# The order of the three split products in a projection, and the place of one wait, in a fused attention and feed-forward kernel

## The reference

```python
x = L0_attn_x
x = x + _layernorm(_L0_attn_ref(_layernorm(x, axis=-1), Wq, bq, Wk, bk, Wv, bv, Wo, bo), axis=-1)
x = x + _layernorm(_L0_ffn_ref(_layernorm(x, axis=-1), ...), axis=-1)
```

## Time and profile before

| | |
|---|---|
| median of 3 runs | 1695.01 us |
| lowest, highest | 1693.71, 1697.49 us |
| the profiled execution, its own time | 1693.71 us |
| its span, first to last instruction | 1691.9 us |
| mean granted TensorE clock | 0.995 |
| TensorE matmuls busy | 1657.7 us, 98% of the span, 22550 matmuls |
| TensorE weight loads busy | 1320.2 us, 78%, 22550 loads |
| DVE, ACT, POOL busy | 1310.4, 855.8, 1284.9 us |

### The profile page before, as it was taken

The page is one execution under the profiler, slowest core; times in us unless marked ns, Lnnn a source line. Parts: engine busy times, 40 slices in busy tenths (PEclk is TensorE's granted clock), DMA queues, the critical chain, the costliest instruction groups (busy, mean ns, idle before and its releaser), DMA issues.

```text
span 1691.9 us, 55468 instructions
## 1 busy us (share of the span) xinstructions
PE 1657.7 (98%) x22550; PEld 1320.2 (78%) x22550; DVE 1310.4 (77%) x2455; ACT 855.8 (51%) x1730; POOL 1284.9 (76%) x1303
## 2 busy tenths in 40 slices
PE   8999999999999999999999999999999999999994
PEld 5787887778787877878787877887788787877873
DVE  7677877778777778778777787787787787777777
ACT  4355554544555555445445445455554554454453
POOL 5577878778778778777787787787787787777867
PEclk9999999999999999999999999999999999999998
DMA  7666666566666666666666666666666666666653
GB/s 266 147 168 166 174 183 175 170 174 189 170 168 183 176 165 181 182 171 169 184 174 170 172 188 173 166 190 172 170 185 175 167 179 180 169 171 173 172 137 95
DMA packets 388635, 293.46 MB, mean 173 GB/s; under 512 B 296854, under 2 KB 296854, under 8 KB 388380
## 3 DMA queue, kind: packets, MB, share of 16 engines
q1 hardware_dynamic: 345552, 223.02, 49.7%
q10 hardware_dynamic: 42828, 66.90, 13.2%
HBM read 155.46 MB, written 67.24 MB: 132 GB/s over the span
## 4 chain that ended last, share of the span: by engine, by line
PE 94%; DVE 2%; issue 1%; DMA 1%; ACT 1%; POOL 1%; ACTq 0%; SPq 0%; DVEq 0%
PE ps_k L1080 8%; PE ps_v L1081 7%; PE ps_v L1083 7%; PE ps_v L1080 7%; PE ps_k L1081 7%; PE ps_y L1161 7%; PE ps_y L1160 7%; PE ps_k L1083 7%; PE ps_y L1164 7%; PE ps_q L1081 7%; PE ps_q L1083 7%; PE ps_q L1080 7%; PE ps_s L1121 6%; PE ps_o L1140 5%; DMA v_key<-v_d 0%
## 5 line engine op out<-in xcount | busy, mean ns | idle before, releaser
L910 ACT ACTIVATE q_sb<-ps_q,mr 128x512 f32<-128x512 f32 x127 | 87.4, 688 | 550.7 <-issue 541.5
L403 POOL TENSOR_TENSOR z<-z,b_row 128x512 f32<-128x512 f32 x124 | 187.7, 1534 | 222.1 <-DVE z L679 222.1
L605 DVE STREAM_TRANSPOSE qT<-q_sb 128x512 f32<-128x512 f32 x128 | 137.5, 1074 | 111.8 <-ACT q_sb L910 111.6
L1080 PE MATMUL ps_k<-wk_hi,xT_hi 128*128 128x512 f32 x504 | 212.1, 421 | 0.0
L1081 PE MATMUL ps_k<-wk_lo,xT_hi 128*128 128x512 f32 x504 | 199.3, 395 | 1.1 <-issue 1.1
L1160 PE MATMUL ps_y<-wo_hi,oT_hi 128*128 128x512 f32 x504 | 199.1, 395 | 0.8 <-ACT oT_hi L926 0.8
L383 POOL TENSOR_TENSOR x_t<-x_t,mr_row 128x512 f32<-128x512 f32 x126 | 195.8, 1555 | 4.6 <-ACT mr_row L1002 4.6
L1081 PE MATMUL ps_q<-wq_lo,xT_hi 128*128 128x512 f32 x504 | 199.3, 395 | 0.0
L1081 PE MATMUL ps_v<-wv_lo,xT_hi 128*128 128x512 f32 x504 | 199.3, 395 | 0.0
L1161 PE MATMUL ps_y<-wo_lo,oT_hi 128*128 128x512 f32 x504 | 199.3, 395 | 0.0
L1080 PE MATMUL ps_q<-wq_hi,xT_hi 128*128 128x512 f32 x504 | 199.1, 395 | 0.0
(11 more groups left out here) (189 smaller groups left out, 3723.4 us busy)
## 6 DMA issues: line engine op xcount, KB each, us to landing
x_in<-in_xa SPq DMA_DIRECT2D x64, 512.0 KB, 5.2
x_t<-in_xt SPq DMA_DIRECT2D x64, 512.0 KB, 4.9
k_bd<-kT SPq DMA_DIRECT2D x512, 64.0 KB, 2.5
v_d<-v_tok ACTq DMA_DIRECT2D x128, 256.0 KB, 2.0
v_key<-v_d SPq DMA_DIRECT2D x128, 256.0 KB, 3.9
res<-in_xr SPq DMA_DIRECT2D x64, 512.0 KB, 5.3
p_bd<-pT ACTq DMA_DIRECT2D x508, 64.0 KB, 2.5
out<-o_sb SPq DMA_DIRECT2D x62, 512.0 KB, 2.9
```

Of the source, the lines that this page charges most:

```text
L403: nc.gpsimd.tensor_tensor(z[:, j, :], z[:, j, :], b_row[:, :], ALU.add).then_inc(z_done, 1)
L605: nc.vector.transpose(qT[t % 2][:, :, :].rearrange("p n h -> p h n"), q_sb[:, :].rearrange("p (h d) -> p h d", d=D)).then_inc(qT_done, 1)
L1080: nc.tensor.matmul(ps, x_hi[:, e, :], w_hi[:, e, :], start=e == 0, stop=False)
```

## The change

`project` loses its second branch: tiles 1 to 127 now take the order that tile 0 had, three passes over the four chunks, hi*hi, then lo*hi, then hi*lo. `output` does the same three passes for tiles 0 to 126, with its wait for oT_lo moved ahead of its first matmul; the last tile (NT - 1) does hi*hi, hi*lo, lo*hi, and waits for oT_lo between the second pass and the third. The number of matmuls, their shapes, operands and banks are the same.

```diff
             def project(t, k, ps, w_hi, w_lo, ready):
                 x_hi, x_lo = xT_hi[t % 2], xT_lo[t % 2]
                 n = order.index(k)
-                if t == 0:
-                    for i, (x, w) in enumerate(((x_hi, w_hi), (x_lo, w_hi), (x_hi, w_lo))):
-                        if i == 1:
-                            pe.wait_ge(first_low, 1)
-                        for e in range(EC):
-                            if e % 2 == 0 and i != 1:
-                                pe.wait_ge(w_split if i else w_cast, 2 * n + e // 2 + 1)
-                            mm = nc.tensor.matmul(ps, x[:, e, :], w[:, e, :], start=i == 0 and e == 0, stop=i == 2 and e == EC - 1)
-                else:
-
+                for i, (x, w) in enumerate(((x_hi, w_hi), (x_lo, w_hi), (x_hi, w_lo))):
+                    if t == 0 and i == 1:
+                        pe.wait_ge(first_low, 1)
                     for e in range(EC):
-                        nc.tensor.matmul(ps, x_hi[:, e, :], w_hi[:, e, :], start=e == 0, stop=False)
-                        nc.tensor.matmul(ps, x_hi[:, e, :], w_lo[:, e, :], start=False, stop=False)
-                    for e in range(EC):
-                        mm = nc.tensor.matmul(ps, x_lo[:, e, :], w_hi[:, e, :], start=False, stop=e == EC - 1)
+                        if t == 0 and e % 2 == 0 and i != 1:
+                            pe.wait_ge(w_split if i else w_cast, 2 * n + e // 2 + 1)
+                        mm = nc.tensor.matmul(ps, x[:, e, :], w[:, e, :], start=i == 0 and e == 0, stop=i == 2 and e == EC - 1)
                 mm.then_inc(ready, 1)
...
                     pe.wait_ge(w_split, 8)
                     pe.wait_ge(vtok_done, 2)
-                o_hi, o_lo, to = oT_hi[t % 2], oT_lo[t % 2], y_bank.get(t, ps_y[:, :])
-                for a in range(EC):
-                    nc.tensor.matmul(to, o_hi[:, a, :], wo_hi[:, a, :], start=a == 0, stop=False)
-                    nc.tensor.matmul(to, o_hi[:, a, :], wo_lo[:, a, :], start=False, stop=False)
-                pe.wait_ge(olo_done, t + 1)
-                for a in range(EC):
-                    mm = nc.tensor.matmul(to, o_lo[:, a, :], wo_hi[:, a, :], start=False, stop=a == EC - 1)
+                if t < NT - 1:
+                    pe.wait_ge(olo_done, t + 1)
+                o_hi, o_lo = oT_hi[t % 2], oT_lo[t % 2]
+                parts = [(o_hi, wo_hi), (o_lo, wo_hi), (o_hi, wo_lo)] if t < NT - 1 else [(o_hi, wo_hi), (o_hi, wo_lo), (o_lo, wo_hi)]
+                for i, (o, w) in enumerate(parts):
+                    if t == NT - 1 and i == 2:
+                        pe.wait_ge(olo_done, NT)
+                    for a in range(EC):
+                        mm = nc.tensor.matmul(y_bank.get(t, ps_y[:, :]), o[:, a, :], w[:, a, :], start=i == 0 and a == 0,
+                                              stop=i == 2 and a == EC - 1)
                 mm.then_inc(y_ready, 1)
```

## The result

The changed kernel took 1704.60 us at the median of its executions (1702.37 to 1708.55), against 1693.72 us (1692.70 to 1697.49) for the kernel before in the same rounds: a ratio of 1.0062, with a 95% interval of 1.0043 to 1.0081. In a second series it was 1698.42 us against 1691.83, ratio 1.0048 (1.0033 to 1.0062). So it is slower by about 0.5%, 7 to 11 us, where no change was forecast.

A forecast was written before the change was run, and what follows sets the result against it. TensorE's matmul stream was taken as the bound. Order, first pair, wait and third semaphore, each 0, left 1693.7 us for the profiled execution; 1.3 more for a median gave 1695.0 us, range 1691.3 to 1698.7.

The forecast's parts named there:

- The order of the matmuls: Changed projection and output blocks, 6096 matmuls: losing repeated stationary chunks costs 0, with 2.4 us either way for rounding.
- The first pair behind a hole: Keys' first two matmuls after the mixing: the same 0.34 us without a shared chunk, taken as 0, at most 1.3 us.
- The rule that the prediction named: Changed blocks: by it, 2032 more loads would cost 380 us if none overlapped; the prediction said no loss here.
- The moved wait: Ahead of the output product, tiles 0 to 126: oT_lo wait 1.87 us earlier, time to spare in every tile, cost 0.
- the 1.89 us to spare: Middle tile: how long oT_lo is finished when the output product's first load starts.
- nothing else is late next: Behind the moved wait: claim that once tile 126 is through, no other wait comes late; size 0.
- The third semaphore: Ahead of the output product: waits grow from two semaphores to three, taken as 0 from the mixing's idle time.
- its rival: Ahead of the output product: a third semaphore costs 0.09 us issue time 127 times, 11 us, 1706 us; chance 0.03.
- The first rival: Output product: the early wait for oT_lo opens a hole in TensorE's stream; example 38 us, 1733 us; chance 0.03.
- bounds of 3.7 us: Order of the matmuls: 2.4 us for spacings plus 1.3 us for keys' first pairs, below and above the forecast.

The follow-up runs named there:

- three quarters of the order alone: New three-pass order in keys, queries and values only, old output product, against the kernel before: 1692.06 us against 1691.83, ratio 0.9996.
- the wait alone: Kernel before with only the oT_lo wait moved ahead of the output product's first matmul, tiles 0 to 126: 1701.46 us, ratio 1.0050; later 1701.99, ratio 1.0059.
- the wait behind the fourth matmul: Kernel before, old order, oT_lo wait behind the output product's fourth matmul instead of eighth, tiles 0 to 126: 1692.16 us against 1693.18, ratio 0.9998.
- the wait for pT: Kernel before plus a wait ahead of the output product's first matmul for the next tile's transposed probabilities: 1699.43 us against 1693.18, ratio 1.0034.

## Why the prediction was wrong

**What bounds the kernel: right.** TensorE's stream, where any hole counts in full. The holes came, only not where the text looked.

**The order of the matmuls, 0: right.** 233.3 ns in all passes after; 0.9996 for three quarters of the order alone, 1.0004 for all of it. The first pair behind a hole is inside the same results. The rule that the prediction named from the Trainium skill (page "TensorE: Matmul & The Clock Gate", section "Step-by-step: what each phase is for"), one load for many matmuls, had no saving to lose here, as argued: there are 22550 loads for 22550 matmuls before and after.

**The moved wait, 0: wrong, and this is the step that failed.** "How long oT_lo is finished when the first load of the output product starts" was measured rightly: no load waits for oT_lo. It is not the time to spare of a wait. The wait is done by TensorE's issue, 3.9 us ahead of the load, so the 1.89 us to spare at the load are 2 us too few at the issue (the hold measured with the wait alone was 1.5 us at the median). The text said that nothing else is late next; what was late next was the transfer of the block of 256 instructions, whose lead over the mixing fell from 6.5 to 2.7 us. The term was 0, and the wait alone measured 9.6 and 8.8 us. The page showed the queue of instruction transfers, and the text left it out.

**The third semaphore, 0: right**, although its rival named 1706 us, near the measured 1704.6. The size was a coincidence: with a third wait that is always met the ratio is 0.9998.

**The first rival** had the right place, the early wait, with the wrong hole: it asked for oT_lo to come 0.84 us later before anything is lost, and gave that 3 in 100. Without any such delay 0.5% was lost.

**The sum and the chances.** With 0.88 on no change, bounds of 3.7 us came from the rounding of the rows. No bound stood for a hold of the issue, so the range could not reach the result.

**What stays open.** What asks for a packet isn't in the records; that it happens only while issue runs is read from when packets start and when they don't. With the wait behind the fourth matmul, too, issue is held until oT_lo is done and has as little time left to the scores' wait as with the wait ahead of the first, and yet the packets start early. That fits if the block has been asked for before that hold, but no run shows the moment; nor does one show why with the wait for pT only half of the packets were late. No kernel was tried in which the borders of the blocks lie elsewhere, or in which the scores' wait is met at once.

## What to carry to other kernels

A wait on an engine that runs its issue ahead has two costs: it can hold the engine, and it can hold the issue. Compare the time at which the awaited result is done with the semaphore instruction's own record, not with the instruction that it guards, and put the wait directly ahead of the first instruction that needs it; four matmuls made the difference between 0.5% and nothing here. Where a dense run of small instructions follows (64 loads and 64 matmuls in 0.8 us), look at the queue of instruction transfers, and at "issue" idle time that cuts a block in the middle.

## What the runs showed of the hardware that was not expected

TensorE's instructions come in blocks of 16 KB, 256 instructions, by transfers of mostly 0.9 to 1.7 us that run among all the others; where TensorE had to wait for one, it went on 1.3 to 1.6 us behind its end. Hardly a transfer starts while TensorE's issue stands at a semaphore (4 of 168 in the kernel before, where such waits fill 18% of the time), and none within 0.86 us behind the end of such a wait. TensorE's issue is about 3.9 us or 17 load and matmul pairs ahead of 128x512 matmuls. Two profiled executions of one kernel differed by 5.5 us, and their mixings by 8.2 us, with transfers that started equally early; over all its executions the changed kernel took 1692.5 to 1708.6 us, with the granted clock at 0.993 to 0.996 in all of them.
